# A new order of adjacency chunks, jobs, attribute sums and projection on TensorE in a two-layer graph network

## What is computed

```python
h = relu(layernorm(x))
xp = (h @ W).reshape(n, 4, 32)
e = leaky_relu(a_s[src] + a_d[dst], 0.2)
e = exp(e - segment_max(e, dst)[dst])
alpha = e / segment_sum(e, dst)[dst]
x = x + relu(segment_sum(alpha * xp[src], dst) + bias)

h = relu(layernorm(x))
edge_agg = segment_sum(edge_attr @ We + be, dst)
x_comb = concatenate([h, edge_agg])
hh = x_comb + segment_sum(x_comb[src], dst)
x = x + relu(hh @ W1 + b1) @ W2 + b2
```

## Time and profile before

| what | before |
|---|---|
| median of 3 runs | 3267.39 us (3266.81 to 3270.06) |
| profiled execution, its own time | 3249.53 us |
| its span | 3247.6 us |
| mean granted TensorE clock | 0.772 |
| busy, share of the span | PE 66%, DVE 57%, POOL 47%, ACT 34% |

### The profile page before, as it was taken

How to read it: one execution, slowest core, us unless ns; L and a number is a source line. 1 busy time by engine, 2 the same in 40 slices (tenths; PEclk the granted TensorE clock), 3 DMA queues, 4 the chain that set the end, 5 groups by cost and what they waited for, 6 DMA issues and landing times.

```text
span 3247.6 us, 60418 instructions
## 1 busy us (share of the span) xinstructions
PE 2133.8 (66%) x16302; PEld 1640.0 (50%) x16302; DVE 1838.2 (57%) x6265; ACT 1095.0 (34%) x2343; POOL 1516.2 (47%) x1625
## 2 busy tenths in 40 slices
PE   4466665665666666656666676666676676667987
PEld 3354554554554545545445454454454445455766
DVE  7365666666666666656556565555555556564221
ACT  3333333333333344333333333333333233332000
POOL 3555555555555555554545555445444444550000
PEclk8666766766767766778878788788888788878999
DMA  9845545555555555565555655556555555655665
GB/s 195 121 137 163 167 139 163 155 153 162 155 153 163 148 165 172 152 182 150 179 153 174 173 170 180 149 162 177 159 153 176 166 147 172 180 138 189 209 198 159
DMA packets 395176, 532.44 MB, mean 164 GB/s; under 512 B 115603, under 2 KB 346723, under 8 KB 383665
## 3 DMA queue, kind: packets, MB, share of 16 engines
q1 hardware_dynamic: 344939, 415.35, 42.4%
q0 software_dynamic: 50112, 115.56, 15.9%
HBM read 385.48 MB, written 145.24 MB: 163 GB/s over the span
## 4 chain that ended last, share of the span: by engine, by line
PE 26%; DVE 21%; another core or an unknown queue 21%; issue 13%; DMA 8%; ACT 5%; SPq 5%; ACTq 1%; DVEq 1%
PE pv L1352 9%; PE pv L1284 5%; PE pt L1275 4%; ACT xsb L942 4%; DVE tabb L1640 4%; DMA state<-zpart 4%; DMA state<-sums 3%; PE pt L1253 2%; DVE big L1932 2%; PE pv L1409 2%; DVE lks L1915 1%; DVE fy L1759 1%; DVE fy L1768 1%; PE pt L1409 1%
## 5 line engine op out<-in xcount | busy, mean ns | idle before, releaser
L906 POOL DMA_INDIRECT big<-table,idx x1566 | 1489.2, 951 | 1372.4 <-issue 399.2
L942 ACT ACTIVATE xsb<-pt 128x343 f32 x1042 | 482.0, 463 | 1547.7 <-remote 922.0
L1253 PE MATMUL pt<-tabb 128*128 128x343 bf16 x1042 | 379.5, 364 | 448.1 <-ACT xsb L942 405.8
L1284 PE MATMUL pv<-big 128*128 128x128 f32 x3132 | 511.3, 329 | 8.0 <-issue 5.6
L1284 PEld LDWEIGHTS pv<-big 128*128 128x128 f32 x3132 | 476.3, 239 | 32.2 <-issue 13.7
L1352 PE MATMUL pv<-big 128*128 128x133 f32 x3132 | 391.6, 280 | 22.2 <-DVE big L1932 22.2
L1253 PEld LDWEIGHTS pt<-tabb 128*128 128x128 bf16 x1042 | 107.9, 104 | 553.8 <-ACT xsb L942 439.9
L1352 PEld LDWEIGHTS pv<-big 128*128 128x128 f32 x3132 | 367.9, 190 | 35.5 <-DVE big L1932 22.4
L1640 DVE TENSOR_TENSOR tabb<-pc,keyp 128x2064 bf16<-128x2064 bf16 x261 | 319.0, 1222 | 0.0
L942 ACT ACTIVATE xsb<-pa 128x343 f32 x521 | 240.9, 462 | 61.8
L1932 DVE TENSOR_TENSOR big<-big,pm 128x768 f32<-128x768 f32 x261 | 233.4, 950 | 30.8 <-ACT pm L942 19.0
(11 more groups left out here) (339 smaller groups left out, 3282.5 us busy)
## 6 DMA issues: line engine op xcount, KB each, us to landing
adj<-xsb SPq DMA_DIRECT2D x87, 1176.0 KB
big<-in_edge_attr_dram SPq DMA_DIRECT2D x87, 1152.0 KB
selb<-rel SPq DMA_DIRECT2D x87, 576.0 KB
pro<-adj SPq DMA_DIRECT2D x28, 896.0 KB
big<-table,idx POOLq DMA_INDIRECT x1566
state<-sums SPq DMA_DIRECT2D x87, 130.5 KB
sums<-state SPq DMA_DIRECT2D x87, 130.5 KB
pro<-adj SPq DMA_DIRECT2D x12, 672.0 KB
```

The costliest lines, as they stand in the source:

```text
L906: pool.indirect_dma_start(out=V[b][:, j, 0:rows], out_offset=None, in_=table, in_offset=bass.IndirectOffsetOnAxis(ap=index[b][:, j:j + 1], ...
L942: return nc.scalar.activation(out_, in_, func, **kw).then_inc(s(name), 1)
L1253: ins = nc.tensor.matmul(to, ohl[:, c, :], ohk[:, c, 0:KW], start=True, stop=alone)
L1284: ins = nc.tensor.matmul(sumA[b], SEL[b][:, j, :], AT[b][:, j, :], start=(j == 0), stop=(j == J - 1))
```

## The change

The constant `FILL`, which cut a job in three, goes; `LEAD` comes: 9 attribute matmuls stand ahead of the look-up in a group without a job, 3 in one with. TensorE's new item: the projection of window n-2, tails, carry back, chunks 9 to 14 of n-1, `mg`, chunks 15 to 17 of n-1, the first LEAD attribute matmuls, the whole job, the look-up, chunks 0 to 2 of n, the other attribute matmuls, chunks 3 to 5, the transposes of window n-1, chunks 6 to 8, sumV. ScalarE follows: chunks 9 to 14 of n-1 ahead of the SEL copy, 15 to 17 behind it, 0 to 2 of n behind `normalise_window`, 3 to 8 behind `fhT`. VectorE's `keep_job` moves from ahead of `pen` to behind the second set of edge marks, and `finish_projection` waits for the transpose of the tails in place of `vm_b`. GpSimd and SP stay as they are. The lines in the program of the change lie 2 to 6 lower than those of the same instructions before (L1253 is L1251).

```diff
@@ -1044,15 +1042,14 @@
                 a(thruT[:, :], thruP, ACT.Copy, "thru_c")
                 if finish_before:
-                    keep_adjacency(n - 1, 1 - b, 15, 18)
+                    keep_adjacency(n - 1, 1 - b, 9, 15)
                 after(act, s("sel_b"), n)
                 if not (isinstance(n, int) and n < 2):
                     act.wait_ge(s("vm_b"), n - 1)
                 a(SEL[b], selH, ACT.Copy, "selc_b")
-                if not is_extra:
-                    after_dma(act, s("adj_out"), n - 1)
-                    keep_adjacency(n, b, 0, 3)
-                else:
+                if finish_before:
+                    keep_adjacency(n - 1, 1 - b, 15, 18)
+                if is_extra:
...
                     normalise_window(n - 1)
                 if not is_extra:
-                    keep_adjacency(n, b, 3, 6)
+                    after_dma(act, s("adj_out"), n - 1)
+                    keep_adjacency(n, b, 0, 3)
...
                     evacuate_window(n - 1)
                 if not is_extra:
-                    keep_adjacency(n, b, 6, 15)
+                    keep_adjacency(n, b, 3, 9)
@@ -1289,16 +1284,16 @@
-                job(n, like, 0, FILL[0])
+                if finish_before and not (isinstance(n, int) and n < 2):
+                    project_window(n - 2)
                 after(pe, s("pre1_b"), n)
                 after(pe, s("thru_c"), n)
                 nc.tensor.transpose(tailT, pre1[:, :, J - 1], ident[:, :]).then_inc(s("tailT_b"), 1)
-                job(n, like, FILL[0], FILL[1])
                 after(pe, s("tails_b"), n)
...
                 if finish_before:
-                    adjacency(n - 1, 15, 18)
+                    adjacency(n - 1, 9, 15)
...
-                job(n, like, FILL[1], NB)
                 after(pe, s("pkl_b"), n)
...
                 ins.then_inc(s("mg_b"), 1)
-                if not is_extra:
-                    adjacency(n, 0, 3, like)
+                if finish_before:
+                    adjacency(n - 1, 15, 18)
...
-                attribute_sums(0, 3)
+                lead = LEAD[1 if parts_of(like) else 0]
+                attribute_sums(0, lead)
+                job(n, like)
...
                 ins.then_inc(s("look"), 1)
                 if not is_extra:
+                    adjacency(n, 0, 3, like)
+                if lead < J:
+                    attribute_sums(lead, J)
+                if not is_extra:
                     adjacency(n, 3, 6)
-                attribute_sums(3, J)
                 if finish_before:
                     transpose_window(n - 1)
...
                 for q in range(QN):
-                    if q == QN - 1 and finish_before:
-                        project_window(n - 1)
                     pe.wait_ge(s("vw_b"), n * QN + (q + 1))
...
                 ins.then_inc(s("vm_b"), 1)
-                if not is_extra:
-                    adjacency(n, 9, 15)
             stage(pe, item)
-            adjacency(NG - 1, 15, 18)
+            project_window(NG - 2)
+            adjacency(NG - 1, 9, 18)
```

More of the change, by code:

```diff
@@ L92 @@
          (82, NG, False))
-FILL = (10, 14)
 PAUSES = ((11, "mg_b"), (14, "look"))
+LEAD = (9, 3)
 TOLD = tuple(c for c in range(J) if c % 3 == 2 or c == J - 2)
@@ L1079, in _ @@
             stage(act, item)
-            keep_adjacency(NG - 1, 0, 15, 18)
+            keep_adjacency(NG - 1, 0, 9, 18)
             normalise_window(NG - 1)
@@ L1238, in project_window @@
                 ins = nc.tensor.matmul(finY, fhT[:, C:2 * C], wew[:, :], start=False, stop=True)
-                if isinstance(m, int) and m == NG - 1:
+                if isinstance(m, int) and m >= NG - 2:
                     ins.then_inc(s("ym_f"), 1)
@@ L1260, in adjacency, with job @@
                         ins.then_inc(s("ab_mm"), 1)
-            def job(n, like, lo, hi):
+            def job(n, like):
                 total = HP * parts_of(like)
-                hi = min(hi, total)
-                if lo >= hi:
+                if not total:
                     return
[L1268 to L1273, removed]
+                if isinstance(n, int):
+                    pe.wait_ge(s("ys2"), parts_of(like))
+                pe.wait_ge(s("aw_in"), n * 16 + (16 - JOB0 * 16))
+                pe.wait_ge(s("ab_ev"), n * J - (J - 15))
+                for i in range(total):
                     q, h = divmod(i, HP)
@@ L1276, in job @@
                                            stop=(i == total - 1))
-                if hi == total:
-                    ins.then_inc(s("jb_mm"), 1)
+                ins.then_inc(s("jb_mm"), 1)
             def item(n, b, it, like=0, is_extra=False):
@@ L1775, in finish_projection @@
             def finish_projection(m):
-                if isinstance(m, int) and m == NG - 1:
-                    dve.wait_ge(s("ym_f"), 1)
+                if isinstance(m, int) and m >= NG - 2:
+                    dve.wait_ge(s("ym_f"), m - (NG - 3))
                 else:
-                    dve.wait_ge(s("vm_b"), m + 2)
+                    after(dve, s("tailT_b"), m + 2)
                 dve.wait_ge(s("y_out"), m * 16 + 16)
@@ L1873, in item @@
                     y_part(Y_LOAD.index(like - 2), 0)
-                keep_job(n, like)
                 after(dve, s("mg_b"), n)
@@ L1912, in item @@
                     edge_marks(n, 1)
+                    keep_job(n, like)
                 after(dve, s("look"), n)
```

## The result

The changed kernel takes 4040.21 us (median of 4 runs, 4035.66 to 4046.79) against 3267.85 (3266.81 to 3270.06): a ratio of 1.2364, 95% interval 1.2343 to 1.2385. It is slower by 772 us. Its profiled execution has a span of 4044.9 us at a mean granted clock of 0.719; before it was 3247.6 at 0.772.

What follows compares the result with a forecast made beforehand. No engine is full; handing over costs time, with GpSimd's gathers as the group's clock and TensorE's signals read late. 37 × 7.6 = 281, 45 × 12.3 = 554 and 20 on 3249.5 give 4105 us, range 3480 to 4290.

Steps and rivals of the forecast that it cites:

- item 4: Chunks 6 to 8 ahead of sumV: they wait for evictions behind `fhT`, and sumV with them; +7.6 us a plain group.
- item 3: Chunks 15 to 17 behind `mg` and the SEL copy: signal 16 held, `look` read at 21.4 us against 20.9.
- held in plain groups too: Rival, chance 0.20: signal 14 is also read late, at 15.6 us; +11.2 us a plain group, 4240 us.
- item 5: Job groups: signal 11 held, so chunks 9 to 14 delay `mg`; +12.1 us with 4 parts, mean +12.3.
- item 2: A job's matmuls move behind `mg`, ahead of `look`: 4.3 to 8.7 us there, 5.8 as a mean.
- item 6: VectorE's moved job reduction, front evictions of 9 to 14, SP's queue: counted at nothing, each under 1 us if uncovered.
- item 1: Six attribute matmuls and the projection leave the stretch between `look` and sumV's end: a gain of 1.7 to 3 us.
- The rule weighed: The skill's rule that PE and ACT never wait on anyone: by it no signal is held, giving 3844 us.
- the first rival: Nothing is held in job groups: they take on average 6.5 us more instead of 12.3; 3844 us, chance 0.20.
- signs of being right: TensorE idle 3 us or more behind the transposes, sumV in one stretch, `look` at about 21 (job: past 30), `pen` past 18.
- signs of being wrong: Chunk 8 early, chunk 17's wait under 1 us, signals 11 and 14 read promptly, job periods growing no more than plain.

Runs made afterwards that it cites:

- edits of `PAUSES`: GpSimd's first stop ahead of gather 8 instead of 11: in the changed kernel 3757.93 us, in the kernel before 3328.45 us (ratio 1.0255).
- the kernel with the lead of eight: Kernel before with the projection moved to the item after next and eight attribute matmuls, not three, ahead of job-less groups' look-up: 3289.18 us, ratio 1.0051.

## Why the prediction was right

The time (4105 forecast, 4040 measured) is within 65 us. The large term and its mechanism were right; that the number is so close is in part luck, for two errors of opposite sign help it. By the profiled executions the 37 plain groups took 357 us more where 281 were forecast, the 45 job groups 413 where 554 were, and the rest 27 where 20 were.

- *Chunks 6 to 8 ahead of sumV* (item 4): right, with its size. The transposes are read at 31.6 us into a plain group, three evictions stand behind `fhT`, TensorE is idle for 5.33 us, and sumV of eighteen runs in one stretch of 5.6 (6.5 taken). It is shown by taking it out (−541) and by putting it in alone (+535).
- *Clock*: right that it falls in the wait. Rows after it show 0.50, then a mean of 0.80.
- *Chunk 17 and the lead* (item 3): the step that failed for plain groups. I had signal 14 read at once and only 16 held, so the look-up at 21.1 us after sumV's end. In the 29 plain groups from 3 to 31, all in a loop, the period is over 40 us, since signal 14 is held (984.52 in the group shown): look-up at 24.5. The seven written out, 32 to 38, take 35.1 to 39.6 us; their signal 14 is read 1.9 to 4.1 us after it is raised. So +9.6 on average over groups 2 to 38 instead of +7.6. This was the rival "held in plain groups too", which had +11.2.
- *Signal 11 in job groups* (item 5): the other step that failed. It was to be held; it was read at once, `mg` was issued at 12.9 us, and only signal 14 was held (2636.58 is 16.5 us in). The look-up was read at 28.5 us instead of 31.8: +9.2 on average instead of +12.3. The place of signal 11 had moved earlier, as its rival said. I had carried over the held signal of a group whose front was filled by a job that the change takes away.
- *The job* (item 2): 28 matmuls took 5.4 us (2642.35 to 2647.79), 5.8 taken.
- *At nothing* (item 6): VectorE's moved reduction, 0.56 us from 2648.09, ends where the look-up's reader starts and delays it by 0.2 us at most. The evictions of chunks 9 to 14 are not covered by the wait for the state's load: TensorE now stands 444.5 us ahead of the carry back (43.5 before), these chunks stand behind it, and the first is evicted 8.4 us into a group, at 976.43. What this costs was not isolated. The projection is a small gain, as item 1 had it.
- *The rule weighed*: with the edits of `PAUSES` in two kernels the late readers moved with the gathers' end, and the first rival, which the prediction drew from the rule, is out by 196 us. What the Trainium skill states there ("SBUF — State Buffer", "Who interferes with whom") is about ports; it says nothing of signals, and no run here tests it.
- *The signs*: of the signs of being right, TensorE's wait behind the transposes and sumV in one stretch came. The others did not. Counted from gather 0, as the prediction counts, `look` was read at 24.4 us in the plain group shown, not at about 21, and at 27.7 in the job group, not past 30; `pen` in the job group came at 15.9, not past 18. Of the signs of being wrong, one came: the period in job groups grew by no more than in plain ones (9.2 against 9.6).

Of the 772 us, some 540 are thus the eviction chain with its clock, and some 40 the lead. The rest, roughly 190 net of the projection's gain, I put down to the later start of the lead and the job, behind evictions whose signal is read late. That last part is argued and not shown: each edit meant to take it away moved the late reading elsewhere.

## What to carry to other kernels

Before a filler is put ahead of critical work on an in-order engine, follow what frees its buffer: here three chunks of 0.3 us drew eighteen matmuls behind a wait that belonged to another window. Look on both engines, for the harm was done equally by the evicting engine's order alone. Where a signal is read promptly only in part of a stage, note at which time it is raised: chunk 16, done 0.7 us later, let its evictions begin 8 us later. And where one stage's code runs partly in a loop and partly written out, read a group of each kind: one timeline and one mean hid here that an edit gained in one kind and lost in the other.

## What the runs showed of the hardware

Signals of TensorE to ScalarE, VectorE and GpSimd that were raised late in a run of indirect gathers were, in groups of the loops, read only some 2 us after the run ahead of a stop had ended. In the groups shown it was 2.2 us after gather 10 (984.52 against 982.28), 2.6 in one group of the kernel with the lead of eight (831.06 against 828.44), 1.9 after gather 7 (897.78 against 895.91), and 1.35 after gather 13. Signals raised up to about 8 us into the first run were read at once, and two in the early part of a later run, 0.4 and 3.1 us after its start, were read while gathers still went out (both with the stop ahead of gather 8). In groups written out, ScalarE read signal 14 at 12.3 to 15.7 us into the group, in loops at 15.8 to 16.7; VectorE read `mg` at 16.5 to 16.8 in both. So where a group's code stands matters, and the plain groups of one kernel have periods of 41 us and of 37.

Signals of ScalarE to TensorE showed no such delay: in the group shown with chunks 6 to 14 behind sumV, TensorE started 0.14 us after the end of `thruT` (842.07 against 841.93), 10.5 us into a run of gathers, while its own next signal was read at 847.22, with VectorE idle for 8.81 us. What holds the others, and why less so in code that is written out, was not tried, and stays open.
